# A routing-and-convolution kernel over 16 images: two passes one after the other, or side by side in a hand-written order

## What is computed

```python
xc = conv2d(group_norm(x), conv1_w, conv1_b)       # 32 groups; 768 -> 16 channels, 1x1
h = mean(xc, axis=(2, 3)) @ H_w.T + H_b            # 4 logits a sample
g = softmax(h, the two largest of 4 only)
for i in range(4):                                 # resize up by 2**i, 3x3 conv, resize down
    experts.append(down(conv2d(up(xc, 2 ** i), convl_w, convl_b)))
out = x + conv2d(sum(g * experts), conv2_w, conv2_b)   # 16 -> 768 channels, 1x1
```

## Time and profile before

| | |
|---|---|
| median of three runs | 1702.09 us |
| span of the profiled execution (its own time is not given apart from it) | 1703.1 us |
| TensorE busy, first instruction to last | 1399.3 us (82%) |
| VectorE busy | 1188.5 us (70%) |
| ScalarE busy | 528.5 us (31%) |
| GpSimd busy | 8.1 us |
| moved by the DMA engines | 593.24 MB, mean 348 GB/s |

### The profile page before, as it was taken

How to read it: one execution, slowest core, us unless ns; L and a number is a source line. 1 busy time by engine, 2 the same in 40 slices (tenths; PEclk the granted TensorE clock), 3 DMA queues, 4 the chain that set the end, 5 groups by cost and what they waited for, 6 DMA issues and landing times.

```text
span 1703.1 us, 28023 instructions
## 1 busy us (share of the span) xinstructions
PE 1399.3 (82%) x9584; PEld 991.1 (58%) x9584; DVE 1188.5 (70%) x3092; ACT 528.5 (31%) x1028; POOL 8.1 (0%) x28
## 2 busy tenths in 40 slices
PE   2799999999999999788897688778768767868862
PEld 2566666666666666466665466556556555656652
DVE  6988888788879887657666656655665664655642
ACT  3577777677777777300000000000000000000000
POOL 0000000000000001000000000000000000000000
PEclk7899999999999999889999898889799879879876
DMA  9888888788888882049999999999999999999999
GB/s 361 315 302 315 313 316 315 275 315 304 298 312 317 301 317 93 1 176 410 416 415 415 417 415 415 417 415 412 415 414 411 403 402 402 402 405 410 399 409 367
DMA packets 203029, 593.24 MB, mean 348 GB/s; under 512 B 10290, under 2 KB 10290, under 8 KB 202932
## 3 DMA queue, kind: packets, MB, share of 16 engines
q1 hardware_dynamic: 202932, 591.95, 89.3%
HBM read 390.60 MB, written 201.33 MB: 348 GB/s over the span
## 4 chain that ended last, share of the span: by engine, by line
PE 48%; DMA 28%; SPq 13%; DVE 6%; issue 3%; ACT 1%; DVEq 0%; ACTq 0%
PE xT_ps L403 22%; DMA out<-x_low 19%; PE img_ps L413 13%; DMA x_low<-in_x 9%; SPq L321 7%; SPq L265 6%; PE img_ps L473 5%; PE xT_ps L500 3%; DVE x_low L867 3%; PE xT_ps L501 2%; PE misc_ps L423 2%; DVE stats L678 2%; ACT xc L559 1%; ACT xT L533 0%; DVE taps L822 0%
## 5 line engine op out<-in xcount | busy, mean ns | idle before, releaser
L867 DVE TENSOR_TENSOR x_low<-x_low,xT_ps 128x768 f32<-128x768 f32 x512 | 470.2, 951 | 322.5 <-PE xT_ps L501 191.0
L500 PE MATMUL xT_ps<-b,all_one 128*128 128x512 f32 (+1 forms) x1024 | 430.5, 424 | 205.3 <-DVE x_low L867 204.6
L533 ACT COPY xT<-xT_ps 128x1024 f32<-128x1024 f32 x384 | 387.4, 1009 | 174.3 <-PE img_ps L413 172.2
L678 DVE BATCH_NORM_STATS2 stats<-x_low 128x6 f32<-128x192 f32 x1320 | 355.9, 344 | 68.6 <-DMA x_low<-in_x 51.4
L500 PEld LDWEIGHTS xT_ps<-b,all_one 128*128 128x128 f32 x1024 | 226.3, 221 | 281.0 <-DVE x_low L867 232.4
L501 PE MATMUL xT_ps<-w,es 128*128 128x512 f32 (+1 forms) x1024 | 376.6, 384 | 0.0
L403 PE MATMUL xT_ps<-ident,x_low 128*128 128x128 f32 x2112 | 291.9, 283 | 24.8 <-DMA x_low<-in_x 11.5
L403 PEld LDWEIGHTS xT_ps<-ident,x_low 128*128 128x128 f32 x2112 | 235.1, 143 | 117.2 <-ACT xT L533 60.4
L599 ACT ACTIVATE es_hi<-img_ps,bias_es 128x512 fp32r<-128x512 f32 x16 | 11.0, 688 | 799.1 <-PE img_ps L473 799.1
L501 PEld LDWEIGHTS xT_ps<-w,es 128*128 128x128 f32 x1024 | 231.5, 226 | 30.6
L473 PE MATMUL img_ps<-xc,band 128*128 (+6 forms) x1120 | 219.4, 343 | 4.2 <-DVE band L828 4.2
(11 more groups left out here) (105 smaller groups left out, 432.5 us busy)
## 6 DMA issues: line engine op xcount, KB each, us to landing
x_low<-in_x SPq DMA_DIRECT2D x208, 1536.0 KB, 11.8
out<-x_low SPq DMA_DIRECT2D x128, 1536.0 KB, 18.0
x_high<-in_x SPq DMA_DIRECT2D x40, 1536.0 KB, 9.9
x_high<-in_L_conv_conv_w SPq DMA_DIRECT2D x8, 48.0 KB, 10.2
bias<-in_L_conv_conv_b SPq DMA_DIRECT2D x8, 0.1 KB, 9.9
wl_raw<-in_L_conv_convl_w SPq DMA_DIRECT2D x8, 9.0 KB, 1.9
bias_l<-in_L_conv_convl_b SPq DMA_DIRECT2D x8, 0.1 KB
gate_w<-in_L_conv_H_w SPq DMA_DIRECT2D x8, 0.2 KB
```

The source lines that it names most:

```text
L500: nc.tensor.matmul(add_ps[:, n % 2, part], all_one[:, :], b2[:, part], start=True, stop=False)
L533: nc.scalar.copy(xT[:, n % XT], xT_ps[:, n % XT_PS]).then_inc(xT_copied, 1)
L678: ins = nc.vector.bn_stats(stats[:, c % STATS_BUFS, g, :], tiles[:, :, g * CG:(g + 1) * CG])
L867: nc.vector.tensor_tensor(slot(i)[:, q, :], slot(i)[:, q, :], add_ps[:, n % 2, :], ALU.add).then_inc(added, 1)
```

## The change

- **One stream of 22 units** (`UNITS`) takes the place of the two passes. A unit (a, b) projects sample a and makes the outputs of sample b. Four units have only an a, then four have both, two only an a, six have both, and six have only a b. Samples are taken in the order 4, 8, 12, 0, 1, 2, 3, 9, 13, 5, 6, 7, 14, 10, 11, 15 for a.
- **The gates come in four rounds** of four samples (`row_due`), the first after the first four images.
- **Half of ten samples stays** (`KEPT`): four of the eight slots are not loaded again. 128 first loads, 88 second loads and 128 stores are left: 344 transfers of 1536 KB, where there were 376.
- **The transfers' order is a table** (`TRANSFERS`): L is a first load, R a second load, S a store, with sample.part:slot. A load waits until the slot's last use is over (transposed, or stored), a store until four tiles are added.
- **In a unit with both**, the sums of the moments of chunks 0 to 2 come first, then the convolution of b with its bands. VectorE takes the last chunk's moments of a in that time, the last sum stands between the convolution's fifth and sixth part (`LATE_SUM_PART`), and the fold of a comes ahead of the low half of b. Then TensorE goes through 12 pairs of steps: two transposes and two projections of a, and two to four tiles of b between them. The following sample's first three chunks of moments come in pairs 6 to 11.
- **Transposes run two steps ahead** (`LEAD` 2, four buffers of `xT`), and transposes, tiles and spreads share one ring of three PSUM buffers (`ring_ps`).
- **Bands and taps are made on GpSimd**, with a ring of four bands, of which the convolution gives one back after each of its seven parts. The experts' taps are set up there too.
- **ScalarE takes 4 of the 32 groups**, not 2.
- **The last bias is in the expansion's matmul**: `es4` has 64 rows of data and 64 of ones, and `w2` the bias in its lower rows, so a tile takes two matmuls and not four. The spread takes 16 matmuls of 64x512 a sample, not 8 of 128x512.

```diff
-XT = 6
-LEAD = KB
-GV = G - 2
+RING = 3
+XT = 4
+LEAD = 2
+BANDS = 4
+GV = G - 4
+UNITS = [(4, None), (8, None), (12, None), (0, None), (1, 0), (2, 1), (3, 2), (9, 3), (13, None), (5, None),
+         (6, 5), (7, 6), (14, 7), (10, 4), (11, 10), (15, 11), (None, 15), (None, 8), (None, 9), (None, 12),
+         (None, 13), (None, 14)]
+KEPT = {s: 4 for s in (0, 1, 2, 3, 5, 6, 7, 10, 11, 15)}
+TRANSFERS = """
...
+S0.0 R0.4:6 R0.5:7 S0.1 L2.0:10 S0.2 R0.6:4 S0.3 L2.1:5 S0.4 R0.7:11 L2.2:8 L2.3:9 S0.5
+L2.4:6 S0.6 L2.5:7 S0.7 L2.6:4 L2.7:11 S1.0 R1.4:4 R1.5:11 S1.1 L3.0:0 S1.2 R1.6:6 S1.3
...
+    for u, (a, b) in enumerate(UNITS):
...
+        if due is not None:
+            pe.append(("logits", due))
+            act.append(("exponent", due))
+            dve.append(("softmax", due))
+            dve.append(("gates", due))
+        if is_late:
+            for c in range(CHUNKS - 1):
+                pe.append(("sum", a, c))
+            statistics(a, CHUNKS - 1, range(GV))
+            fold(a)
+        if due is not None:
+            pe.append(("gates", due))
+        if b is not None:
+            for part in range(NM):
+                pe.append(("conv", b, part))
+                if is_late and part == LATE_SUM_PART:
+                    pe.append(("sum", a, CHUNKS - 1))
+            act.append(("high", b))
+            dve.append(("low", b))
+            for part in range(2):
+                spread(b, part)
+        if is_late:
+            for n in range(LEAD):
+                transpose(a, n)
...
+            def store(s, i):
+                kind = source[s, i]
+                n = loads[kind][0]
+                stores[n] += 1
+                sp.wait_ge(added, BI[s] * TILES + (i + 1) * QN)
+                sp.dma_start(out_v[s, i // 4, i % 4], x_sb[:, n]).then_inc(stored[n], 16)
...
+            for bi, b in enumerate(B_ORDER):
+                pool.wait_ge(gates_ready, b // 4 + 1)
+                if bi:
+                    pool.wait_ge(band_ready, NM * bi)
+                    pool.wait_ge(band_used, NM * bi - BANDS + 1)
+                weigh_taps(b, bi)
+                for part, m in enumerate(MAT_ORDER):
+                    n = NM * bi + part
+                    if n >= BANDS and part:
+                        pool.wait_ge(band_used, n - BANDS + 1)
+                    full = [P, NT, NH, R]
+                    nc.gpsimd.tensor_tensor(band[:, n % BANDS], taps[:, MAT_ROW_TAP[m]].unsqueeze(2).broadcast_to(full),
+                                            masks[:, MAT_MASK[m]].unsqueeze(1).broadcast_to(full),
+                                            ALU.mult).then_inc(band_ready, 1)
```

More of the change, by code:

```diff
@@ new lines, in tiles_by_pair, with groups_by_pair @@
+def tiles_by_pair(u):
+    b = UNITS[u][1]
+    if b is None:
+        return [0] * (STEPS // 2)
+    last = TILE_PAIRS if KEPT.get(b, 0) else TILE_PAIRS_LOADED
+    ends = [min(TILES, -(-TILES * (m + 1) // last)) for m in range(STEPS // 2)]
+    return [end - start for start, end in zip([0] + ends, ends)]
+def groups_by_pair(u):
+    a, following = UNITS[u][0], (UNITS[u + 1][0] if u + 1 < len(UNITS) else None)
+    out = [[] for _ in range(STEPS // 2)]
+    if following is None or a is None:
+        return out
+    chunks = 3 if late(u + 1) else 4
+    b = UNITS[u][1]
+    first = 0 if b is None else GROUPS_FROM if KEPT.get(b, 0) else GROUPS_FROM_LOADED
+    last = 12 if late(u + 1) else 11
+    every = [(c, g) for c in range(chunks) for g in range(GV)]
+    for n, item in enumerate(every):
+        out[first + n * (last - first) // len(every)].append(item)
+    return out
@@ new lines, with psum_turns, image_places @@
+PE_ORDER, ACT_ORDER, DVE_ORDER = orders()
+def psum_turns():
+    turn = {}
+    for work in PE_ORDER:
+        if work[0] in ("transpose", "tile", "spread", "weights_2", "logits"):
+            turn[work] = len(turn)
+    return turn
+TURN = psum_turns()
+TURNS = list(TURN)
+def image_places():
+    place, before, free, held = {}, {}, [(n, None) for n in range(XC)], {}
+    for a, b in UNITS:
+        if b is not None:
+            free.append((held.pop(b), b))
+        if a is not None:
+            place[a], before[a] = free.pop(0)
+            held[a] = place[a]
+    return place, before
@@ L718, in fold_norm @@
[L718 to L725 removed]
+                dve.wait_ge(deviation_ready, AI[a] + 1)
@@ new lines, in _ @@
+            for work in DVE_ORDER:
+                if work[0] == "groups":
+                    groups(*work[1:])
+                elif work[0] == "add":
+                    add(*work[1:])
+                elif work[0] == "fold":
+                    fold(*work[1:])
+                elif work[0] == "low":
+                    low_half(*work[1:])
+                elif work[0] == "softmax":
+                    softmax(*work[1:])
+                elif work[0] == "gates":
+                    take_gates(*work[1:])
+                elif work[0] == "weights_1":
+                    weights_1()
+                else:
+                    weights_2()
```

1110 lines of the change are left out of this document (585 added, 525 removed).

## The result

The changed kernel takes **1791 us** (median) against 1702 us for the kernel before on the same chip: 1.0537 times as long, 95% interval 1.0515 to 1.0559. It is slower, as I thought likeliest, but by 89 us instead of 23, and one microsecond above my range. The profiled execution has a span of 1788.1 us. A mark is the first store of a sample, as in the prediction.

A forecast was written before the change was run, and what follows sets the result against it. Before the change TensorE set pass A and transfers pass B. Following the queue between first stores, 269.5 + 620 + 109.3 + 109.2 + 210 + 82 + 326 = 1726, forecast 1725 us against 1702; forecast's own range 1700 to 1755, overall range 1660 to 1790.

The forecast's parts named there:

- The seven gaps: In units with both samples, the queue is empty for some 27 us, seven times, with all twelve slots taken.
- the full tail: From S15.0 to the end 84 transfers are left and the queue stays full: 326 us.
- the start: From the kernel's start to the first store S0.0, TensorE alone sets the pace: 269.5 us.
- My own sign of being wrong: Wrong if first stores are over 108 us apart, dips much under 20 us or missing, or a slot takes 3.66 us.
- the six intervals that were to be 103.4: First store to first store in six units with both samples: 103.4 us each, 620 us together.
- A: Rival: slots move faster when the queue is refilled, below 3.71 us each, giving 1691 us; chance 0.27.
- B: Rival: units overlap as busy times allow, 76.2 us a unit, seven gaps of 27 less, giving 1536 us; chance 0.10.
- the paragraph on GpSimd: Taps and bands on GpSimd: 7.5 us between a round's gates and convolution; other samples' bands covered by the loop, costing nothing.
- The fold's own term: Fold of the late sample on the chain behind the last load: 4.2 us, between bounds of 2.3 and 5.2.
- Taps and first band before a round's convolution: Seven operations of 400 elements and the first band on GpSimd after a round's gates: 7.5 us, upper estimate 8.7.
- S4.0 to S10.0: Interval with a round: additions, held by the loads, end at 63, then moments, softmax, taps, convolution and store: 109.2 us.
- Rival C: More waits: GpSimd slow in rounds and ring of four bands (4 x 8 us), half clock behind gaps: 1792 us; chance 0.13.

The follow-up runs named there:

- e1: Changed kernel, but GpSimd's tap weighing and bands for the next sample wait until the late sample's fold is done: 1762 us, ratio 1.0358.
- e9: Changed kernel with GpSimd waiting for the fold before weighing the next taps, and VectorE weighing the taps of each round's first sample: 1743 us, ratio 1.0260.
- e6: Changed kernel, but VectorE instead of GpSimd weighs the taps of the first sample of each round: 1776 us, ratio 1.0455.
- e3: Changed kernel with the early sample's whole convolution, spreads and four tiles ahead of the late sample's sums and fold in ten units: 1803 us, ratio 1.0608.
- e4: Like e3, but eight tiles ahead of the fold, transfers at a unit's start reordered and GpSimd's next-sample work behind the fold: 1792 us, ratio 1.0533.
- e7: Changed kernel with transfers, moments, tiles and convolution reordered in ten units, GpSimd waiting for the fold, VectorE weighing rounds' first taps: 1682 us, ratio 0.9898.

## Why the prediction was wrong

- **Structure: right.** The seven gaps, the queue's 20 transfers, the waits for `added` and the full tail (328 against 326) came as said; the start was forecast ten too long (269.5 against 260), which hid a part of the rest. My own sign of being wrong came too: four of the six intervals that were to be 103.4 are over 108, at 111.5 to 112.3. Rivals A and B are out: slots went at 3.9 us each (81.2 us from S0.0 to the last landing, 79.2 forecast), and no unit overlapped.
- **The failing step** is in the paragraph on GpSimd: the other samples' bands "are made while TensorE and the transfers are busy with the loop of pairs, some 50 us, and cost nothing". GpSimd doesn't wait for the loop: it weighs the next taps as soon as this sample's seventh band is made (348.05, 0.16 us behind it) and the convolution has given back a buffer, and that is the time of the fold. I looked for cover in time and not for what the two engines share. The fold's own term was right: 4.2 against 3.77 without GpSimd, 8.0 with it. Seven times 4.24 us is 29.7, and e1 gave 29 back. With the rounds' taps off GpSimd as well (e9) the time is 1743, within the 1700 to 1755 that I gave the forecast, though with the start's 9.5 us in its favour.
- **Taps and first band before a round's convolution**: 10.6 us against 7.5, even above my upper bound of 8.7, 12 us in four rounds. The bound took one pass for every input and output at the fill's rate; seven operations took 8.8 us (1.28 us for one input, 1.03 for two) and the band 1.53. *The estimate from the Trainium skill (GPSIMD Engine Reference, section Elementwise), 5.6 us, was further off still, and my arithmetic was wrong: the page's 4.5 us for 2048 elements, scaled by size to the 3440 elements of these eight operations, is an estimate of 7.6 us.*
- **The units without slow folds** are 107.3 against 103.4. In the one to S3.0 the last load landed 2.0 us late, the sum came 1.0 later, the fold was 0.4 shorter, and from the end of the low half to the store 11.4 us passed instead of 9.9 (12.3 in the unit to S1.0). In this last stretch TensorE, idle for 2.6 us before, runs the spreads 0.43 us apart instead of 0.23, at a granted clock of 0.74 from 579 to 585.5 us. I had priced the clock at nothing here and only in rival C.
- **S4.0 to S10.0** is 127.5 against 109.2. The additions of sample 4 ended 72 us after S4.0 and not 63: 8.8. Further, 3.1 are GpSimd's, 4.2 lie between the first matmul of the convolution and the end of the low half (the fold with GpSimd beside it), and 2.7 between that and the store. VectorE stood idle for 15.6 us before tiles of sample 4 (the row is shown with e6), because their second load is the eleventh transfer behind S4.0. These are the queue's waits from 1141 to 1225 us:

```profile
SPq L495 <- DVE x_sb L1002: 28.1, 8, 12.5
SPq L486 <- DMA out<-x_sb: 20.5, 4, 7.0
```

Its waits for transposes are 4.7 us there. I had let additions be "held by the loads" without following the queue.
- **Rival C** gave 1792 and came nearest, but by luck. GpSimd in the rounds and the low clock are in it, the clock at 5 us a gap where 1.5 to 2.3 were measured. One of its two large terms, GpSimd slow in the ring of bands (32 us), didn't occur: TensorE waited for a band four times, 45.2 us in all, only in the rounds. The slow fold isn't in it.

Together: start -9.5; six intervals +42; S3 to S5 +5; S4 to S10 +18; the others +6: 62 us above the sum of 1726. What of that is not fold or GpSimd in the rounds is read from the changed kernel's rows; no run took those terms away one by one.

## What to carry to other kernels

Work moved to an idle GpSimd is not free even when nobody waits for it: ask which chain of small VectorE operations with two SBUF inputs it will lie beside, and make it wait until that chain is done if that chain is what the next store waits for. In a unit that is a chain through a full set of buffers, moving one piece ahead only moved the waiting elsewhere (e3, e4); it took a new order of the transfers and of every engine's program together to win (e7). And a saving in busy time (179 us here) is worth only what lies on the chain (24 us).

## What the runs showed of the hardware

A VectorE operation with two inputs in SBUF, of 0.16 to 0.25 us on 1 to 96 elements, that began 0.03 to 0.17 us after a two-input operation of GpSimd ended 0.02 to 0.12 us behind it: it took 0.90 to 1.00 us beside GpSimd operations of 1.03 us and 1.61 us beside one of 1.52 us. There are 28 such cases in the seven slow folds of the changed kernel. That it is held until GpSimd's operation ends is my reading of these two lengths; no run varied the length on purpose. Beside a one-input operation of GpSimd two such operations took 0.3 to 0.4 us more, and others nothing; which it will be stays open. Additions with an input in PSUM, and moments, were not slowed. GpSimd took longer for one input times a scalar (400 elements, 1.28 us) than for two inputs (1.03 us). VectorE needed 0.43 and 0.58 us for the same in e6.
